# Reordering the prologue and the first sequences of a fused adaLN transformer block

## The reference, cut to what matters

```
mod = silu(c) @ wmod -> sa, ca, ga, sb, cb, gb        # one row of 128 each per sequence
ga, gb: magnitude at least 0.25, sign kept
h = layernorm(x) * (1 + ca) + sa
x = x + ga * attention(h)     # 16 heads of 8, keys within 32 tokens, biases bq bk bv bo
h = layernorm(x) * (1 + cb) + sb
x = x + gb * ffn(h)           # router softmax, top 2 of 8 experts, plus a shared expert
```

## Time and profile before

| what | us |
|---|---|
| median of three timed runs | 700.81 |
| the three runs | 700.81, 695.68, 701.35 |
| the profiled execution | 696.14 |
| its span, first to last instruction | 694.1 |
| start of the first scores in it | 37.91 |

### The profile page before, as it was taken

How to read it: one execution, slowest core, us unless ns; L and a number is a source line. 1 busy time by engine, 2 the same in 40 slices (tenths; PEclk the granted TensorE clock), 3 DMA queues, 4 the chain that set the end, 5 groups by cost and what they waited for, 6 DMA issues and landing times. The chain is left out here.

```text
span 694.1 us, 19396 instructions
## 1 busy us (share of the span) xinstructions
PE 653.3 (94%) x6075; PEld 560.8 (81%) x6075; DVE 599.7 (86%) x1568; ACT 554.5 (80%) x2458; POOL 566.2 (82%) x667
## 2 busy tenths in 40 slices
PE   6488889999999999999999999999999999999897
PEld 5277777888888888888888888888888888887685
DVE  6737778999898989999999999899989999897685
ACT  3258787989888888989898889899899898986352
POOL 6430619999988979899998989898999999898684
PEclk8669988999999999999999999999999999999999
DMA  5567788786787787786878777887868787633231
GB/s 175 157 143 192 164 211 219 197 232 165 178 241 196 202 219 190 189 231 159 224 205 227 190 201 205 228 201 191 201 190 210 207 209 221 157 101 99 77 129 31
DMA packets 193862, 127.79 MB, mean 184 GB/s; under 512 B 110640, under 2 KB 170720, under 8 KB 193632
## 3 DMA queue, kind: packets, MB, share of 16 engines
q1 hardware_dynamic: 193760, 126.56, 69.2%
HBM read 96.36 MB, written 30.17 MB: 182 GB/s over the span
## 5 line engine op out<-in xcount | busy, mean ns | idle before, releaser
L1184 ACT ACTIVATE p<-ps_s,nmx 128x96 f32<-128x96 f32 x1024 | 330.9, 344 | 34.9 <-DVE nmx L1738 33.0
L1184 ACT ACTIVATION_READ_ACCUMULATOR p<-ps_s,nmx 128x1 f32 x1024 | 216.2, 211 | 0.0
L737 POOL TENSOR_TENSOR xs<-h,sbc 128x512 f32<-128x512 f32 x128 | 165.5, 1300 | 18.9 <-DMA sbc<-s_scr 17.6
L1738 DVE TENSOR_REDUCE nmx<-ps_s 128x4 f32<-128x384 f32 x256 | 137.2, 548 | 37.0 <-PE ps_s L2697 36.8
L2697 PEld LDWEIGHTS ps_s<-k,q 128*128 128x128 f32 x1024 | 140.1, 197 | 34.1 <-DMA k<-k_scr 14.2
L743 POOL TENSOR_TENSOR xl<-xs,xh 128x512 fp32r<-128x512 f32 x120 | 153.4, 1283 | 17.2 <-ACT xh L1206 17.1
L2697 PE MATMUL ps_s<-k,q 128*128 128x96 f32 x1024 | 145.4, 277 | 18.7 <-DMA k<-k_scr 13.3
L2765 PE MATMUL ps_Y<-w2s,g 128*128 128x128 f32 x1152 | 153.5, 279 | 0.4 <-DVE g L1844 0.4
L2765 PEld LDWEIGHTS ps_Y<-w2s,g 128*128 128x128 f32 x1152 | 140.4, 192 | 5.6 <-DVE g L1844 0.8
L1755 DVE STREAM_TRANSPOSE pt<-p 128x384 f32<-128x384 f32 x256 | 133.5, 551 | 0.8 <-ACT p L1184 0.3
L1206 ACT ACTIVATE xh<-xs 128x512 fp32r<-128x512 f32 x128 | 79.9, 636 | 34.0 <-POOL xs L737 33.5
(11 more groups left out here) (138 smaller groups left out, 1010.8 us busy)
## 6 DMA issues: line engine op xcount, KB each, us to landing
sbc<-s_scr SPq DMA_DIRECT2D x64, 512.0 KB, 6.2
k<-k_scr SPq DMA_DIRECT2D x64, 384.0 KB
q<-q_scr SPq DMA_DIRECT2D x128, 96.0 KB
k<-k_scr SPq DMA_DIRECT2D x32, 336.0 KB
q_scr<-qh SPq DMA_DIRECT2D x32, 256.0 KB, 3.7
k_scr<-kh SPq DMA_DIRECT2D x32, 256.0 KB, 2.9
xr<-x SPq DMA_DIRECT2D x16, 256.0 KB, 3.1
q_scr<-ql SPq DMA_DIRECT2D x16, 256.0 KB, 3.7
```

Of the source, the lines that this page charges most:

```text
L737: nc.gpsimd.tensor_tensor(xs[:, n % 2], h2[:, par], sbc[:, n - 1], ALU.mult).then_inc(xs_d, 1)
L1184: last = nc.scalar.activation(p[:, n % PRING, gg, :], ps_s[:, n % 2, MK * gg:MK * gg + MK], ACT.Exp, bias=nmx[:, n, gg:gg + 1], accum_out= ...
L1738: nc.vector.tensor_reduce(nmx[:, n, :], ps_s[:, n % 2, 0:ACC].rearrange("p (g k) -> p g k", g=HG), AX.X, ALU.max, negate=True).then_inc(mx ...
```

## The change

SP issues `ct` first, then x of sequence 0, wmod, wqkv and the four small tensors. Each of the large ones has a semaphore of its own (`ct_in`, `wm_in`, `wq_in`), so tanh(c/2) waits for `ct` alone. x of sequence 2 is loaded before the first q is stored. `put_rows` moves behind `load_k(0, 0)`, and `load_bias(0)`, which waits for those rows, comes right after it.

DVE clears a quarter of `q4` instead of a half in its first memsets, takes the statistics of sequence 0 at once, and makes the rows ga, gb, ga*bo (`make_rows`) behind `low_k(0)`. One memset of `k4` moves between `low_h1(0)` and `low_q(0)`. POOL normalises sequence 0 ahead of the first `ones_q`, and takes over the other quarter of `q4` and, in `fill()`, the clearing of its second half. ACT makes tanh and `wqh` before the edge tiles and takes over the second `ones_q`. PE's 14 identity fillers become 8.

In `fill()`, steps change places on every engine within sequences 0 to 4, and there are fewer `warm` matmuls in sequences 0 and 1. `body()` and `drain()` are untouched.

```diff
         def _(sp):
-            sp.dma_start(wqf, wqkv).then_inc(w_in, 16)
-            sp.dma_start(ct[:], cT).then_inc(w_in, 16)
-            sp.dma_start(wm, wmod).then_inc(w_in, 16)
+            sp.dma_start(ct[:], cT).then_inc(ct_in, 16)
+            sp.dma_start(xr[:, 0], x[0:1].rearrange("o (a p) d -> p (o a) d", p=128)).then_inc(x_in[0], 16)
+            sp.dma_start(wm, wmod).then_inc(wm_in, 16)
+            sp.dma_start(wqf, wqkv).then_inc(wq_in, 16)
...
-            load_x(0)
             sp.dma_start(w13f, w13).then_inc(e_in, 16)
             sp.dma_start(w2f, w2).then_inc(e_in, 16)
             load_x(1)
             def fill():
-                put_rows()
+                load_x(2)
                 put_q(0, 0)
                 put_ql(0, 0)
                 put_k(0, 0)
                 put_kl(0, 0)
                 load_q(0, 0, 0)
                 load_k(0, 0, 0)
+                put_rows()
                 load_bias(0)
                 load_ga(0)
                 load_q(0, 1, 0)
                 load_k(0, 1, 0)
-                load_gb(0)
-                load_bias(1)
-                load_x(2)
...
         # POOL
-            ones_q(0)
+            spread_var(0, l1, ln1)
+            inverse(0, l1, ln1)
+            shift(0, l1, ln1)
+            normal(0, l1, ln1)
+            pool.wait_ge(l1["xn"], NQB)
+            ones_q()
...
-            ones_q(1)
-            spread_var(0, l1, ln1)
-            inverse(0, l1, ln1)
-            shift(0, l1, ln1)
-            normal(0, l1, ln1)
+            nc.gpsimd.memset(q4[0:KROWS, 0, 2:4].bitcast(F32), 0.0).then_inc(z_in[0], 1)
...
         # ACT
+            act.wait_ge(ct_in, 16)
+            nc.scalar.activation(cth[:], ct[:], ACT.Tanh, scale=0.5).then_inc(s_th, 1)
+            act.wait_ge(wq_in, 16)
+            nc.scalar.activation(wqh[:, 0], wqf[:, 0], ACT.Copy, scale=SCALE)
+            nc.scalar.activation(wqh[:, 1:3], wqf[:, 1:3], ACT.Copy).then_inc(s_wh, 1)
             act.wait_ge(cst, IDENT + 3)
...
             def fill():
+                ones_q()
+                copy_w2()
                 copy_w13()
-                copy_w2()
...
         # DVE
-            nc.vector.memset(q4[0:KROWS, 0].bitcast(F32), 0.0).then_inc(z_in[0], 1)
-            nc.vector.memset(k4[KROWS:128, :, :, 1].bitcast(F32), 0.0)
+            nc.vector.memset(q4[0:KROWS, 0, 0:2].bitcast(F32), 0.0).then_inc(z_in[0], 1)
...
             statistics(0, l1, ln1)
             moments(0, l1, ln1)
+            dve.wait_ge(s_th, 1)
+            nc.vector.scalar_tensor_tensor(cth[:], cth[:], 1.0, ct[:], ALU.add, ALU.mult).then_inc(s_sv, 1)
+            dve.wait_ge(s_sv, 1)
+            nc.vector.tensor_scalar(csl[:], cth[:], 0.5, None, ALU.mult).then_inc(s_sl, 1)
+            dve.wait_ge(s_wh, 1)
...
             dve.wait_ge(s_sa, 1)
...
             low_h1(0)
+            nc.vector.memset(k4[KROWS:128, :, :, 1].bitcast(F32), 0.0)
             low_q(0)
             low_k(0)
             def fill():
+                make_rows()
+                turn_v(0)
+                split_w13()
                 statistics(1, l1, ln1)
                 moments(1, l1, ln1)
-                split_w13()
-                turn_v(0)
-                clear_q()
...
         # PE
-            for i in range(14):
+            for i in range(8):
                 mm(ps["A"][:, 0:128], ident[:], ident[:], start=True, stop=True)
-            pe.wait_ge(w_in, 112)
-            pe.wait_ge(s_wh, 1)
+            pe.wait_ge(wm_in, 16)
             pe.wait_ge(s_sl, 1)
...
                 scores(0, 3)
                 flip(1, l1, ln1, "M1")
+                warm(2)
+                scores(0, 4)
+                warm(4)
+                project_q(1)
+                scores(0, 5)
                 warm(3)
-                scores(0, 4)
-                warm(6)
-                scores(0, 5)
-                project_q(1)
+                scores(0, 6)
                 project_k(1)
-                scores(0, 6)
-                warm(5)
+                values(0, 0)
+                values(0, 1)
+                values(0, 2)
                 scores(0, 7)
```

More of the change, by code:

```diff
@@ L456, in fill @@
                 load_k(1, 0, 1)
+                load_bias(1)
+                load_ga(1)
+                load_gb(0)
                 load_q(1, 1, 1)
-                load_ga(1)
+                put_sums(0)
                 load_bias(2)
-                put_sums(0)
                 get_sums(0)
@@ L479, in fill @@
                 load_k(2, 1, 0)
+                load_bias(3)
                 put_q(3, 1)
@@ L516, in fill @@
                 get_sums(3)
+                load_bias(5)
                 load_k(4, 1, 0)
@@ L875, in fill @@
                 expand_v(3, 1)
+                add_bias(4)
                 route_scores(2)
+                gate_wo(3)
                 scaled_low(1, 5, 1)
@@ L904, in fill @@
                 normal(3, l2, ln2)
-                gate_wo(4)
+                add_bias(5)
                 scaled_low(2, 4, 0)
@@ L1227, in expert, with ones_q @@
                 nc.scalar.activation(th[:, par], banks(b, n)[0], ACT.Tanh, scale=0.5).then_inc(th_d, 1)
+            def ones_q():
+                act.wait_ge(cst, IDENT)
+                nc.scalar.activation(q4[KROWS:128, 1].rearrange("p g n j q -> p (g n j) q"),
+                                     ident[KROWS:128, KROWS:128].unsqueeze(1).to_broadcast([MB, HG * HB * HJ, MB]),
+                                     ACT.Copy).then_inc(q_one[1], 1)
             def copy_w13():
@@ L1907, in fill @@
                 maximum(0, 3)
+                low_h1(1)
                 maximum(0, 4)
-                low_h1(1)
                 maximum(0, 5)
@@ L1937, in fill @@
                 maximum(1, 0)
+                statistics(2, l1, ln1)
                 maximum(1, 1)
+                moments(2, l1, ln1)
                 turn_p(0, 15)
-                statistics(2, l1, ln1)
-                moments(2, l1, ln1)
                 turn_p(1, 0)
@@ L1948, in fill @@
                 maximum(1, 4)
+                low_h1(2)
                 maximum(1, 5)
-                low_h1(2)
                 scale_o(0)
@@ L2833, in fill @@
                 scores(0, 14)
-                warm(3)
-                scores(0, 15)
                 values(0, 6)
@@ L2838, in fill @@
                 values(0, 8)
-                warm(2)
-                scores(1, 0)
-                scores(1, 1)
-                turn_sums(0)
-                project_v(1)
                 values(0, 9)
                 values(0, 10)
+                scores(0, 15)
+                warm(5)
+                scores(1, 0)
+                warm(2)
+                turn_sums(0)
+                scores(1, 1)
+                warm(7)
+                scores(1, 2)
+                warm(3)
+                scores(1, 3)
                 values(0, 11)
                 values(0, 12)
+                flip(2, l1, ln1, "M1")
+                scores(1, 4)
+                warm(1)
+                scores(1, 5)
                 values(0, 13)
@@ L2862, in fill @@
                 attn_out(0)
+                scores(1, 7)
                 values(1, 0)
-                scores(1, 7)
-                warm(3)
+                values(1, 1)
+                values(1, 2)
+                values(1, 3)
                 project_k(2)
@@ L2893, in fill @@
                 turn_sums(1)
[L2894 to L2897 removed]
+                values(1, 8)
                 values(1, 9)
@@ L2902, in fill @@
                 values(1, 13)
+                scores(2, 2)
+                scores(2, 3)
+                scores(2, 4)
                 values(1, 14)
@@ L2981, in fill @@
                 scores(3, 10)
-                scores(3, 11)
                 values(3, 2)
@@ L2987, in fill @@
                 values(3, 6)
+                scores(3, 11)
                 router(2, 0)
@@ L3017, in fill @@
                 values(3, 15)
+                down(1, 6, 1)
+                scores(4, 3)
                 expert(1, 8)
```

305 lines of the change are left out of this document (139 added, 166 removed).

## The result

| | median us | lowest to highest | executions |
|---|---|---|---|
| before | 698.32 | 695.68 to 701.35 | 4 |
| after | 689.73 | 688.07 to 690.25 | 4 |

The profiled execution took 690.25 us (span 688.5), against 696.14 (694.1).

A forecast was written before the change was run, and what follows sets the result against it. Engines feed each other from the second sequence, so the gain is how much earlier first scores start: 696.14 - 6.5 = 689.6 us, other terms zero, plus 2 of the 4.7 to the median: 691.5. Range 685 to 699.

The forecast's parts named there:

- rival E: Sequences 0 and 1: fewer fillers leave PE gaps, the clock falls, 4 us per stretch, four give 705.6; chance 0.09.
- Steps 1 to 3: Prologue up to PE's product with mod: inputs land earlier, `csl` ready at 5.7 instead of 11.36, product starts at 8.6.
- Step 4: From the product with mod to `hh`: fuller clock saves 0.85 of 5.25 us, `hh` at 13.0, 6.5 us earlier.
- Step 5: From `hh` to the first scores: 18.4 us as before, the work moved into it costing zero.
- Step 6: SP's queue: rows land at 32, `load_q(0, 1)` issued near 33.2; zero cost, 3.5 us to spare at `scores(0, 8)`.
- Rival D: Second half of sequence 0's q and k loads comes late, giving 692 to 694; chance 0.10.
- step 7: Reordered steps of sequences 0 to 4: taken as 0, bounds of 3 us either way.
- rival C: The first sequences also shrink, by the full 3 us of step 7, giving 686.5; chance 0.17.
- A: Gain is the 6.5 us earlier start: 688 to 691 like the profiled execution, 688 to 695 with scatter; chance 0.47.
- F: The start moves earlier but a later constraint gives it back, leaving 696; chance 0.05.

The follow-up runs named there:

- E2: The new prologue with the old order of steps and old fillers in sequences 0 to 4: 691.18 us, ratio 0.9899 to the kernel before.
- E10: E2 with six fillers ahead of `scores(0, 8)`: 688.48 us, ratio 0.9889 to the kernel before.
- E9: The kernel before with six fillers ahead of `scores(0, 8)`: 694.25 us, ratio 0.9959 to the kernel before.
- E3: The old prologue with the new order of steps and fewer fillers in sequences 0 to 4: 693.64 us, ratio 0.9941 to the kernel before.
- E1: The changed kernel once more, with no edit: 688.08 us, ratio 0.9859 to the kernel before.
- E5: The changed kernel with `put_rows` moved ahead of `load_k(0, 0)`: 688.03 us, ratio 0.9877 to the kernel before.
- E12: E7 plus 3, 3, 5 and 8 fillers ahead of tiles 2 to 4 of sequence 2 and sequence 3's transposes: 683.30 us, ratio 0.9809.
- E7: The changed kernel with six fillers ahead of `scores(0, 8)`: 684.92 us, ratio 0.9834 to the kernel before.
- E11: The changed kernel with six fillers ahead of `scores(0, 10)` instead, behind the wait: 688.57 us, ratio 0.9887 to the kernel before.
- E8: The changed kernel with 52 fillers before the first scores, six before `scores(0, 8)`, and 3, 3, 5 in sequence 2: 685.02 us, ratio 0.9837.
- E6: The changed kernel with 52 fillers ahead of the first scores, in PE's wait for k loads: 686.27 us, ratio 0.9851 to the kernel before.
- E4: The changed kernel with POOL's first cast into `q4` moved ahead of normalising sequence 0: 690.66 us, ratio 0.9899 to the kernel before.

## Why the prediction was right, and where not

The time, 691.5, is 1.8 us over the median, and the 689.6 worked out for an execution like the profiled one is 0.65 us under the profiled 690.25. The gain of 8.6 us lies just above the one per cent (7 us) that the prediction drew as its line, on the side to which it gave 0.36. The path was right: the earlier `csl` made the first scores 6.43 us earlier (6.5 taken), and with the old order (E2, E10 against E9) the prologue is worth 6.5 and 5.8 us. What followed was not zero, and that the profiled time came within 0.65 us is luck: errors cancelled. The lead in the profiled executions moved like this:

- At the first scores it was 6.4 us, at `scores(0, 8)` 8.0. E2, with the old order, gains the same 1.5 us there. In the kernel before the granted clock was 0.50 up to 48.3 us (the earlier trace rows has 39 to 47 us), in the changed kernel up to 38.3.
- At `scores(0, 14)` it was 5.0. The longer fall of the clock took 2.9 (see rival E below).
- At `put_scores(0)` it was 8.5. These 3.5 us are the new order's: E3 gains 2.9 in the same stretch, and E2 loses 0.3.
- At `put_scores(4)` it was 8.7, at `put_scores(15)` 5.8, and the spans differ by 5.6. So the loop took 2.9, and why is open.

**Steps 1 to 3: right.** `x` was at DVE at 4.32 (4.0 taken), wqkv at ACT at 6.02 (6.3), `csl` was ready at 5.87 (5.7), the product with `mod` at 8.78 (8.6). The statistics did go onto the path, and the long operation of DVE went when the cast was moved. One term was left out: PE also waits for wmod, which landed at 5.31 here but later than `csl` was ready in four other executions of this prologue (E1, E2, E5, E12: 5.8 to 6.3 us), where PE's wait ends with it, as both lines below show. It cost up to 0.4 us.

**Step 4: mechanism right, its clock term too large.** `hh` came at 13.69, not 13.0. From the product with `mod` to `hh` took 4.91 us against 5.25 before: 0.34 of the 0.85 taken, as the product took 1.46 and the three fillers 1.33, both as in the earlier trace rows. Those are the durations of the half clock, so it did not stay full here. The rest of the 0.7 is the 0.2 us by which the product with `mod` came late. This term isn't a constant. In two other executions of the same prologue the same two lines read so, E12 first and then the changed kernel again (E1):

```profile
6.38 1.06 PE L2655 MATMUL ps_M<-csl,pt 128*128 128x16 f32 x8 [0.93 <-DMA pt<-wmod]
...
12.80 0.69 ACT L1167 ACTIVATE hh<-ps_M,mod 128x512 fp32r<-128x512 f32 x1 [1.50 <-PE ps_M L2678]
```

```profile
5.96 1.89 PE L2650 MATMUL ps_M<-csl,pt 128*128 128x16 f32 x8 [0.51 <-DMA pt<-wmod]
...
13.65 0.69 ACT L1167 ACTIVATE hh<-ps_M,mod 128x512 fp32r<-128x512 f32 x1 [2.75 <-PE ps_M L2673]
```

Over the ten executions of this prologue with the cast in its place, `hh` starts between 11.93 and 14.08, and these matmuls take either 1.03 to 1.06 or 1.86 to 1.89 us.

**Step 5: right.** From `hh` to the first scores took 17.8 us (18.4 taken), which gave back most of what step 4 had lost. The memset of `k4` (1.76 us, from 15.64), POOL's half of `q4` (1.80, from 13.96) and the second `ones_q` on ACT (3.62, from 17.63) cost nothing.

**Step 6: right.** `load_q(0, 1)` was issued at 32.7 (33.2 taken), no DMA wait stands ahead of `scores(0, 8)`, and E5, with the second half 3.4 us earlier, was no faster. Rival D is out. That the rows wait behind the large loads was read rightly: they landed at 31.8 (32 taken), 4.7 us behind their issue, against 1.4 in the kernel before and 2.0 in E5.

The Trainium skill, "DMA: Bandwidth & Descriptors", section "Queues, rings and completion order", was cited against this step for order in the queue. The 4.7 us against 1.4 agree. So does E2, where the store of `rst` took its 5.1 us behind two broadcast loads, against 3.2 without them: the rule bears on step 7, where the prediction did not look.

**Step 7: mis-sized.** I took 0 with bounds of 3 either way, because PE and ACT are busy in sequence 1. It is 3 to 4 us: 4.0 by E3, 3.1 from E1 and E2, 3.6 from E7 and E10. (The order takes out 10 of the 100 fillers of `fill()`; the prediction had 11 of 93.) This is rival C, at 0.17, and it came true along with A. What failed in this step was the argument from busy shares. The waits behind `put_sums(0)` and `get_sums(0)` in SP's queue were not read, though they end a wait of DVE and one of PE. How much of the 3 to 4 us hangs on them is open.

**Rival E: mechanism right, size not decisive.** The clock does fall in sequence 0, behind the 1.31 us wait of the earlier trace rows which I had listed as evidence against it. What a fall costs can be read from the start of `scores(0, 8)` to that of `scores(0, 14)`. It is 8.7 us in all seven profiled executions without a fall, with the six fillers or not. It is 9.6 and 9.8 with 3.4 us at half clock (the kernel before, E1), 11.3 with 6.8 us (E3, E5), and 12.5 and 12.7 with 10.2 us (the changed kernel, E2). (E11 has six more fillers in the stretch: 10.8 with 3.4 us.) So the profiled execution of the changed kernel paid 3.8 us and that of the kernel before 0.9. The difference of 2.9 us is most of what lies between the 5.9 us of the two profiled executions and the 8.6 to 9.6 of the medians. But over many executions the kernel before pays too. Filling the gap brings 2.5 us there (E9) and 1.7 to 3.2 in the changed kernel (E7). The two can't be told apart, so the change added nothing measurable to an old cost, where the rival wanted several new stretches of 4 us.

**The 4.7 us between the profiled execution and the median before.** I wrote that nothing in the rows tells why, and put 2 of them on the forecast. The new medians of the kernel before are 696.05 to 697.67, at most 1.5 us above the profiled 696.14. So 2 was too much, and the 4.7 came from having three executions only. A good part of the scatter goes with the gap. The five kernels with the six fillers in it spread over 1.4 to 4.0 us (E7 1.4, E8 2.5, E10 3.5, E9 3.7, E12 4.0), the seven without them (E1 to E6, E11) over 5.2 to 7.8, and the kernel before beside them over 7.3 to 10.4. What makes the stretch long or short from one execution to the next is not known.

**F, a later constraint gives it back**: in part. Between `put_scores(4)` and `put_scores(15)` the lead falls by 2.6 to 2.9 us, with the granted clock at 1.00 in both kernels. No experiment separates what takes it.

## What to carry to other kernels

Before costing a reordering at nothing because the engines are busy, follow each short store and its read-back through the queue: a 16 KB store behind two loads that nobody needs yet came back 2 us later. Where TensorE waits after a dense stretch (1.26 to 1.33 us here), look at the granted clock behind the wait. Here six filler matmuls inside that wait brought 2 to 3 us, and the same six behind it nothing. And compare several executions of one kernel before explaining a difference of 3 us between two profiles.

## What the hardware showed that was not expected

- **The clock falls after a short wait, for a varying time.** Behind a wait of 1.26 us at `scores(0, 8)`, the half clock lasted 10.2 us in one profiled execution of the changed kernel, and behind 1.27 us only 3.4 in another (E1). Without fillers in that wait it occurred in seven of nine profiled kernels (not in E4 and E6); with them in none of five (E7 to E10, E12).
- **The view of the clock misses a half rate at the start.** In the changed kernel's 11 to 12 us it reads 1.00, and E12's 0.50, while in both the three fillers took 1.33 us, as in the earlier trace rows. The trace's first entry for the clock, a rise to 1.00, is at 14.4 us in the changed kernel and at 5.9 in E12, and what lies ahead of it is shown as 1.00. In the five executions of this prologue whose first entry comes at 14 us or later (the changed kernel, E1, E4, E5, E7) the product with `csl` took 1.86 to 1.89 us, in the six where it comes before 6.1 us it took 1.03 to 1.06. So in the first group TensorE ran at the half clock all the way to `hh`. In the prologue the durations of matmuls of one shape are the better witness.
- **POOL's cast holds a DVE operation with two SBUF inputs to its own end.** E4's `wql` (2.54 us against 0.29) ended 0.15 us after the cast. The wait shows as the operation's own duration and not as idle time. `bqk`, with one input in PSUM and one in SBUF, took 0.23 us at 10.36 in the changed kernel, in the middle of the cast. The Trainium skill, "SBUF — State Buffer", section "Who interferes with whom", calls this an exclusive lock: a DVE instruction with two SBUF inputs contends with a GpSimd instruction that reads SBUF, one with at most one does not. Both rows agree.
